# Two layers of a gated cross-attention block: Toeplitz rows of four heads read straight from kernel_rev, and two units with memory of their own

## The reference, cut to what matters

```python
def _L0_xattn_ref(k, v, q, ssm_kernel, D, head_dim):       # k = v = ctx, q = layernorm(x)
    kv = jnp.einsum('bhil,bhjl->bijhl', k_, v_)
    y = irfft(rfft(kv, n=fft_size) * rfft(ssm_kernel, n=fft_size))[..., :L]
    out = y + kv * D[None, None, None, :, None]
    out = jnp.einsum('bijhl,bhil->bjhl', out, q_)
...
x = x + jnp.tanh(g_xattn[0]) * _L0_xattn_ref(ctx_2048, ctx_2048, _layernorm(x), ssm_kernel, D, 8)
x = x + jnp.tanh(g_ffn[0]) * _L0_ffn_ref(_layernorm(x), ...)
x = x + jnp.tanh(g_xattn[1]) * _L1_xattn_ref(_layernorm(x), ctx_2048, mask)
x = x + jnp.tanh(g_ffn[1]) * _L1_ffn_ref(_layernorm(x), w_fc, w_proj)      # square(relu(x w_fc)) w_proj
```

## Time and profile before

| | |
|---|---|
| median of 3 runs | 231.15 us (230.76 to 231.24) |
| the profiled execution | 230.63 us, span of its instructions 228.9 us |
| TensorE busy | 217.5 us, 95% of the span, 1405 matmuls |
| VectorE busy | 177.5 us, 78% |
| ScalarE, GpSimd busy | 111.2 us, 49%; 77.7 us, 34% |
| granted TensorE clock, mean | 0.989 |
| DMA | 14068 packets, 11.46 MB |

### The profile page before, as it was taken

The page is one execution under the profiler, slowest core; times in us unless marked ns, Lnnn a source line. Parts: engine busy times, 40 slices in busy tenths (PEclk is TensorE's granted clock), DMA queues, the critical chain, the costliest instruction groups (busy, mean ns, idle before and its releaser), DMA issues.

```text
span 228.9 us, 4229 instructions
## 1 busy us (share of the span) xinstructions
PE 217.5 (95%) x1405; PEld 198.7 (87%) x1405; DVE 177.5 (78%) x507; ACT 111.2 (49%) x221; POOL 77.7 (34%) x113
## 2 busy tenths in 40 slices
PE   7679899999999999999999999999999999998994
PEld 7579899998889889889889898889989988998883
DVE  4289999988989978698986597873587638846874
ACT  2341367942355343746353573494932682435443
POOL 2279998376553321010130343200101211201530
PEclk9799999999999999999999999999999999999998
DMA  5699953000000007000000000000000100001011
GB/s 170 138 292 345 325 172 111 3 0 3 0 1 3 0 0 229 3 1 0 3 0 0 3 0 0 3 3 0 0 3 0 46 0 3 0 6 44 0 47 46
DMA packets 14068, 11.46 MB, mean 50 GB/s; under 512 B 2944, under 2 KB 13792, under 8 KB 14048
## 3 DMA queue, kind: packets, MB, share of 16 engines
q1 hardware_dynamic: 11792, 11.03, 15.7%
q10 hardware_dynamic: 2256, 0.18, 0.7%
HBM read 10.14 MB, written 1.07 MB: 49 GB/s over the span
## 4 chain that ended last, share of the span: by engine, by line
PE 76%; DMA 8%; DVE 8%; ACT 2%; POOL 2%; issue 2%; ACTq 0%; SPq 0%; DVEq 0%; POOLq 0%
PE bank L808 25%; PE bank L646 12%; PE bank L838 6%; PE bank L812 4%; PE bank L873 4%; PE bank L889 4%; PE bank L836 3%; PE bank L693 3%; DMA ctx<-in_ctx_rows 3%; PE bank L694 3%; PE bank L695 3%; DMA lag_rows<-lags 2%; PE bank L639 2%; DMA toe<-lag_rows 2%; PE bank L725 1%
## 5 line engine op out<-in xcount | busy, mean ns | idle before, releaser
L808 PE MATMUL bank<-w_split,xt 128*128 128x512 f32 (+1 forms) x288 | 66.3, 378 | 0.0
L808 PEld LDWEIGHTS bank<-w_split,xt 128*128 128x128 f32 x288 | 51.5, 188 | 7.0 <-issue 0.2
L1352 DVE SCALAR_TENSOR_TENSOR act<-silu,scal,bank 128x176 f32<-128x176 f32 (+2 forms) x80 | 23.7, 355 | 17.1 <-ACT silu L1044 17.1
L1044 ACT ACTIVATE silu<-bank 128x512 f32<-128x512 f32 (+1 forms) x24 | 13.5, 563 | 28.8 <-PE bank L812 28.7
L838 PE MATMUL bank<-d_split,a_t 128*128 128x512 f32 x70 | 24.9, 396 | 0.0
L1513 POOL TENSOR_TENSOR fold<-prod 128x512 f32<-128x512 f32 x16 | 20.7, 1296 | 11.6 <-DVE att L1211 7.6
L898 ACT ACTIVATE a_t<-bank 128x512 fp32r<-128x512 f32 (+1 forms) x24 | 13.4, 559 | 19.8 <-PE bank L646 16.4
L561 POOL TENSOR_TENSOR kv<-ctx_ext 128x640 f32<-128x640 f32 x15 | 19.5, 1306 | 9.7 <-ACT ctx_ext L898 4.0
L836 PE MATMUL bank<-d_split,a_t 128*128 128x256 f32 x77 | 20.5, 281 | 0.0
L1454 POOL TENSOR_SCALAR ve<-mv 128x2 f32<-128x2 f32 (+2 forms) x11 | 3.1, 280 | 49.6 <-DVE mv L1134 49.6
L1099 DVE TENSOR_TENSOR a_t<-bank,a_t 128x512 fp32r<-128x512 f32 (+1 forms) x24 | 15.3, 639 | 3.5 <-ACT a_t L898 3.5
(11 more groups left out here) (162 smaller groups left out, 466.3 us busy)
## 6 DMA issues: line engine op xcount, KB each, us to landing
toe<-lag_rows SPq DMA_DIRECT2D x3, 512.0 KB, 7.5
ring<-in_down_p SPq DMA_DIRECT2D x2, 704.0 KB, 5.0
ctx<-in_ctx_rows SPq DMA_DIRECT2D x2, 512.0 KB, 6.7
ring<-in_gate_p SPq DMA_DIRECT2D x2, 512.0 KB, 7.1
ring<-in_up_p SPq DMA_DIRECT2D x2, 512.0 KB, 5.9
out_x<-x_res SPq DMA_DIRECT2D x3, 256.0 KB, 2.1
tern_w<-in_w_fc SPq DMA_DIRECT2D x1, 640.0 KB, 4.4
tern_w<-in_w_proj SPq DMA_DIRECT2D x1, 640.0 KB, 5.6
```

What stands on the lines that cost most here:

```text
L808: pe.matmul(psum((name, b, c))[:, 0:w_cols], lhs, w_split[:, w, kt, part, cols], start=i == 0, stop=False)
L1044: drain(act_e.activation(silu[:, n % 2, 0:w_cols], psum(("gate", b, c))[:, 0:w_cols], ACT.Silu), ("gate", b, c))
L1352: drain(dve.scalar_tensor_tensor(out=act[:, whole], in0=silu[:, n % 2, here], scalar=scal[:, b, g:g + 1], in1=psum(("up", b, c))[:, here], ...
```

## The change

It does five things.

1. `toe` of heads 0 to 3 (`DIRECT = 2` groups of two heads) is read from `kernel_rev` itself and without waiting. DVE adds D to it afterwards: `add_skip(k)` takes the identity with its columns reversed, times D of the head (`skip_all`, a new load to all partitions), plus the half of `toe` that holds lag zero. `add_skip(0)` stands on DVE ahead of the first norm, `add_skip(1)` behind its kv 0 0. The twelve other heads go the old way.
2. Loads are moved: gate0 and gate1 of the ring stand behind heads 4 to 7 and 8 to 11; `mu` and the router's weights are issued by ScalarE after its part of turn_q 0 0. `lags` is loaded ahead of `skip_sb`.
3. GpSimd's kv 0 1 waits for DVE's kv 0 0, and its first fold for the store of `lag_rows`.
4. Units 3 and 4 get `hid_late` and `x1t_late` of their own, in the memory of `w_split`, and wait for the last chunk instead of for the unit before.
5. `TIMES` has new numbers. Up to the first products the list now has conv 0 0 to 0 5 ahead of the first `turn_w`, and then turn_w gate 0 to 3 in a row; mu_hi and mu_lo stand around conv 0 12; turn_ctx 1 0 stands after turn_w up 3; the third keep (4 matmuls) stands ahead of mask_up up 1 and no longer after conv 1 2. At the end hidden 2 1 stands ahead of down 7, turn_p 3 ahead of the statistics of unit 4, read 3 ahead of turn_0 4, turn_1 4 between hidden 3 1 and 3 2, all hidden pieces of unit 4 ahead of out 3, and the last keep behind out 4.

```diff
+DIRECT = 2
...
+LATE_UNIT = 3
...
-    "weights": [13, 20, 28, 30, 36, 37, 45, 55, 56, 57, 58, 61, 62, 67, 68, 69, 72, 75, 80, 87, 88, 101, 123, 125,
-        126, 127, 137],
...
-    "mu": [14, 15],
-    "mix1": [50, 53, 70, 83, 91, 93],
-    "kv0": [12, 19, 29, 32, 41],
-    "conv0": [16, 17, 21, 22, 24, 26, 33, 34, 38, 39, 47, 48, 51, 59, 63, 65],
-    "gather0": [25, 31, 44, 46, 54, 64, 76, 77],
...
-    "keeps": [74, 81, 106, 109, 110, 322],
...
-    "unit2": [262, 263, 266, 268, 273, 276, 277, 278, 280, 292, 299, 303, 309],
-    "unit3": [282, 285, 290, 295, 300, 304, 307, 308, 311, 315, 316, 319, 323],
-    "unit4": [297, 298, 302, 306, 310, 312, 313, 314, 321, 324, 326, 328, 330],
...
-    "low2": [294, 301, 305],
-    "low3": [317, 318, 320],
-    "low4": [325, 327, 329],
+    "weights": [26, 27, 28, 29, 33, 42, 44, 45, 51, 52, 63, 64, 65, 66, 67, 72, 73, 74, 82, 91, 92, 103, 122, 123,
+        127, 128, 138],
...
+    "mu": [48, 50],
+    "mix1": [56, 57, 75, 83, 94, 95],
+    "kv0": [19, 20, 23, 36, 40],
+    "conv0": [12, 13, 15, 16, 18, 21, 30, 31, 34, 37, 39, 46, 49, 60, 62, 68],
+    "gather0": [24, 25, 35, 41, 54, 55, 77, 78],
...
+    "keeps": [58, 76, 81, 109, 110, 330],
...
+    "unit2": [261, 262, 266, 269, 273, 279, 280, 281, 287, 292, 295, 301, 309],
+    "unit3": [284, 286, 289, 296, 298, 302, 305, 306, 311, 315, 317, 319, 328],
+    "unit4": [299, 300, 307, 308, 310, 312, 313, 314, 318, 322, 324, 325, 329],
...
+    "low2": [293, 303, 304],
+    "low3": [316, 320, 321],
+    "low4": [323, 326, 327],
...
-            assert at["out", u - 1] < at["hidden", u, 0]
+            if u < LATE_UNIT:
+                assert at["out", u - 1] < at["hidden", u, 0]
+            else:
+                assert at["hidden", u - 1, 2] < at["hidden", u, 0] and at["hid_lo", u - 1, 2] < at["hid_lo", u, 0]
+                assert at["chunk", B - 1, NPART - 1] < at["turn_1", u]
...
-    w_split = sb("w_split", [P, 2, 2, 2, GI], F32R)
+    split_at = region(4 * 8 * GI)
+    w_split = sb("w_split", [P, 2, 2, 2, GI], F32R, split_at)
...
+    hid_late = [sb(f"hid_late{k}", [P, JT, 2, P], F32R, split_at + 4 * JT * 2 * P * k) for k in range(2)]
+    x1t_late = [sb(f"x1t_late{k}", [P, 2, 2, P], F32R, split_at + 4 * JT * 4 * P + 4 * 4 * P * k) for k in range(2)]
+    hid_of = [hid_t, hid_t, hid_t] + hid_late
+    x1t_of = [x1t, x1t, x1t] + x1t_late
...
+    skip_all = sb("skip_all", [P, HEADS])
...
+    skip_spread, toe_skip = sem("skip_spread"), sem("toe_skip")
...
-            ring_load(0)
-            sp.wait_ge(lags_stored, 16)
             for k, hs in enumerate(TOE_LOADS):
...
-                src = bass.AP(lag_rows.tensor, hs.start * KPAD, [[1, P], [KPAD, len(hs)], [1, 256]])
+                if k == DIRECT:
+                    sp.wait_ge(lags_stored, 16)
+                rows = kernel_rev if k < DIRECT else lag_rows
+                src = bass.AP(rows.tensor, hs.start * KPAD, [[1, P], [KPAD, len(hs)], [1, 256]])
                 sp.dma_start(toe[:, hs.start:hs.stop, :], src).then_inc(toe_loaded[k], 16)
-                if k == 2:
-                    ring_load(1)
+                if k >= DIRECT and k < DIRECT + 2:
+                    ring_load(k - DIRECT)
             ring_load(2)
...
                     if half == 0:
-                        pe.wait_ge(toe_loaded[next(k for k, hs in enumerate(TOE_LOADS) if h in hs)], 16)
+                        k = next(k for k, hs in enumerate(TOE_LOADS) if h in hs)
+                        if k < DIRECT:
+                            pe.wait_ge(toe_skip, k + 1)
+                        else:
+                            pe.wait_ge(toe_loaded[k], 16)
...
-                                                 fc_t[:, kt, j * P:(j + 1) * P], x1t[:, part, kt, 0:n],
+                                                 fc_t[:, kt, j * P:(j + 1) * P], x1t_of[u][:, part, kt, 0:n],
...
-                                                 hid_t[:, j, part, k * P:(k + 1) * P],
+                                                 hid_of[u][:, j, part, k * P:(k + 1) * P],
...
+            act_e.dma_start(lags[:, :], kernel_rev).then_inc(lags_loaded, 16)
             act_e.dma_start(skip_sb[:, :], skip.unsqueeze(1)).then_inc(lags_loaded, 16)
-            act_e.dma_start(lags[:, :], kernel_rev).then_inc(lags_loaded, 16)
+            act_e.dma_start(skip_all[:, :], skip.partition_broadcast(P)).then_inc(skip_spread, 16)
...
             act_e.wait_ge(lags_made, 1)
             act_e.dma_start(lag_rows, lags[:, :]).then_inc(lags_stored, 16)
-            act_e.dma_start(router_w[:, :], gate_w).then_inc(small_loaded, 16)
-            for kt in range(2):
-                act_e.dma_start(mu[:, kt, :].rearrange("p (g s) -> p g s", g=NG),
-                                mask_up_w[:, kt * P:(kt + 1) * P, :].rearrange("g h s -> h g s")).then_inc(mu_loaded, 16)
...
+                    if step == ("turn_q", 0, 0):
+                        for kt in range(2):
+                            act_e.dma_start(mu[:, kt, :].rearrange("p (g s) -> p g s", g=NG), mask_up_w[:, kt * P:(kt + 1) * P, :]
+                                            .rearrange("g h s -> h g s")).then_inc(mu_loaded, 16)
+                        act_e.dma_start(router_w[:, :], gate_w).then_inc(small_loaded, 16)
...
-                        wait_filled(act_e, ("hidden", u - 1, 2))
+                        wait_filled(act_e, ("up", B - 1, NPART - 1) if u >= LATE_UNIT else ("hidden", u - 1, 2))
...
-                    drain(copy(x1t[:, 0, :, 0:n], psum(step)[:, 0:2 * n].rearrange("p (t n) -> p t n", t=2)), step)
+                    drain(copy(x1t_of[u][:, 0, :, 0:n], psum(step)[:, 0:2 * n].rearrange("p (t n) -> p t n", t=2)), step)
...
-                        wait_filled(act_e, ("out", u - 1) if u else ("turn_proj", 2))
-                    act_e.activation(hid_t[:, j0:j0 + nj, 0, 0:rows], relu[:, n % 2, 0:nj * rows].rearrange(
+                        wait_filled(act_e, ("up", B - 1, NPART - 1) if u >= LATE_UNIT else ("out", u - 1) if u else
+                                    ("turn_proj", 2))
+                    act_e.activation(hid_of[u][:, j0:j0 + nj, 0, 0:rows], relu[:, n % 2, 0:nj * rows].rearrange(
...
+
+            def add_skip(k):
+
+                dve.wait_ge(toe_loaded[k], 16)
+                for h in TOE_LOADS[k]:
+                    last = dve.scalar_tensor_tensor(out=toe[:, h, P:2 * P], in0=ident[:, ::-1], scalar=skip_all[:, h:h + 1],
+                                                    in1=toe[:, h, P:2 * P], op0=ALU.mult, op1=ALU.add)
+                last.then_inc(toe_skip, 1)
...
                 elif kind == "norm" and not by_scalar(*step[1:]):
...
+                    if n == 0:
+                        dve.wait_ge(skip_spread, 16)
+                        add_skip(0)
...
                     make_kv(dve, half, g).then_inc(kv_beside, 1)
+                    if half == 0 and g == 0:
+                        add_skip(1)
...
-                    residue(x1t[:, 1, :, 0:n], step, psum(step)[:, 0:2 * n].rearrange("p (t n) -> p t n", t=2),
-                            x1t[:, 0, :, 0:n])
+                    residue(x1t_of[step[1]][:, 1, :, 0:n], step, psum(step)[:, 0:2 * n].rearrange("p (t n) -> p t n", t=2),
+                            x1t_of[step[1]][:, 0, :, 0:n])
...
-                    dve.tensor_tensor(hid_t[:, j0:j0 + nj, 1, 0:rows],
+                    dve.tensor_tensor(hid_of[u][:, j0:j0 + nj, 1, 0:rows],
...
-                                      hid_t[:, j0:j0 + nj, 0, 0:rows].bitcast(F32), ALU.subtract).then_inc(hid_lo, 1)
+                                      hid_of[u][:, j0:j0 + nj, 0, 0:rows].bitcast(F32), ALU.subtract).then_inc(hid_lo, 1)
...
+                    if half == 0 and g == 1:
+                        pool.wait_ge(kv_beside, 1)
                     make_kv(pool, half, g).then_inc(kv_made, 1)
                 elif kind == "fold":
...
+                    if n == 0:
+                        pool.wait_ge(lags_stored, 16)
```

20 lines of the change are left out of this document (10 added, 10 removed), and 26 rows, old and new, of the table TIMES.

## The result

The changed kernel takes 231.62 us (median of 8 runs, 230.89 to 232.09), the kernel before 230.44 us beside it. The ratio is 1.0052, with a 95% interval of 1.0028 to 1.0076: slower by 1.2 us. The profiled execution took 231.89 us with a span of 230.1 us.

The account below looks back on a forecast made before the run. DVE, without slack from 20 to 28 us behind a hollow start, was taken as the bound up to the logits. Start +0.3 and end -0.35 gave -0.05 us: no change, median 231.1 us, range 229.6 to 232.7.

Parts of the forecast that it names:

- the 9.2 us transfer: First new transfer, Toeplitz rows of heads 0 and 1 (256 KB) behind ctx, forecast to land at 9.2 us.
- the start: Everything up to the logits: gains and new waits of DVE were summed to +0.3 us, bounds -0.5 and +1.3.
- The rest: Everything behind the first chunk; the only term forecast there was the one for the end, -0.35 us.
- the clock: Rival: a new PE hole from 10.3 to 11.3 us keeps TensorE at 1.2 GHz longer; 232.6 us, chance 0.04.
- owed mu_lo: DVE work done in the old start's hollow, still to be done later; about 0.43 us instead of 0.78.
- PE's wait ahead of gate tiles 2 and 3: Tiles need ring load 1, in near 19.5 us; PE idles 1 us or more there, DVE 0.4 us.
- Exclusion: Rival: DVE's adds and GpSimd's kv exclude each other, all DVE work 1.1 us late; 232.2 us, chance 0.2.
- DVE's adds need no semaphore by then: Reason for leaving the hold-up by GpSimd's kv (up to 1.25 us) out of the sum: GpSimd must still receive one.
- the moved small loads would cost: Rival: mu and router loads push the full DMA, ctx of half 1 or ring load 1 1.2 us later; 232.3, chance 0.13.
- DVE is not the limit: Rival: PE keeps its 0.9 us lead at the start and the tail gives 0.35; 229.9 us, chance 0.25.
- The term for the end: Units 3 and 4 and the work around the last down step: -0.35 us, bounds -1.1 and +0.3.
- The waits that I listed: New waits at the end: PE for the qt copy 0.5 us, hidden 4 0 for the copy of x1t 0.3 us.

Follow-up runs that it names:

- spread_pe: Changed kernel with D spread over the partitions on chip (identity scaled by D, matmul with ones) instead of by the skip_all load; ratio to the kernel before 0.9990.
- after_warm: Changed kernel with 13 more warm matmul steps ahead of the first turn of ctx and 4 ahead of turn_q; ratio to the kernel before 1.0038.
- adds_first: Changed kernel with the second pair of adds ahead of DVE's kv 0 0 instead of behind it; ratio to the kernel before 1.0050.
- loads_back: Changed kernel with the loads of mu and router weights back directly behind the taps' write on ScalarE's queue; ratio to the kernel before 1.0055.
- tail_only: Kernel before, with the changed order from down 3 (step 225) on and the own memory of units 3 and 4; ratio to the kernel before 0.9983.
- middle_only: Kernel before, with the changed order only between the first chunk (step 137) and down 3 (step 225); ratio to the kernel before 1.0006.
- mended_ring: spread_pe with both pairs of adds between norm mix 0 and kv 0 0, and ring load 0 ahead of the taps' write wait; ratio to the kernel before 0.9938.

## Why the prediction was wrong

**The step that failed** is the sentence that the new load of skip_all "is waited for by the same instruction as the 9.2 us transfer, which hides it". That is true of it as a wait and false of it as traffic. I priced its bytes at nothing, and let ctx land at 8.5 us and the new transfers behind it at 9.2 and 9.9. They landed at 9.34, 9.99 and 10.95 us, and the taps' write at 10.76 instead of 10.06. In the kernel before the load alone costs 1.5 us, which is more than the whole measured difference.

**The balance.** By the ratios the start costs 0.91%, 2.1 us; without the load (changed kernel to spread_pe, 0.62%) 1.4 us of that go, and 0.7 us stay, for +0.3 forecast. The rest gains 0.4 to 0.8%, 0.9 to 1.9 us, for -0.35 forecast. I put the cost of the start too low and the gain of the rest too low. The two errors partly cancel, and it is luck that 231.62 us lies inside my range of 229.6 to 232.7.

**The start, step by step.** A pair of adds takes 0.61 us (0.65 forecast), and the first pair starts when its rows land, as forecast, but at 10.09 and not at 9.2 us. Norm ends at 11.99 (11.25), turn_q starts at 12.05 (11.3), conv 0 0 at 13.81 (12.7): 0.75 us from the landing, the rest from the clock, since turn_q took 1.97 us and not 1.4. The second pair took 1.66 us. The copy of q_ext ended at 15.70 us (13.9). DVE's owed mu_lo was to cost 0.43 us; it took 1.21, beside GpSimd's fold, in the timeline of the changed kernel:

```profile
32.36 1.21 DVE L1147 TENSOR_TENSOR mu<-mu,mu 128x256 fp32r<-128x256 f32 x1
```

PE's wait ahead of gate tiles 2 and 3 did not appear; it did in after_warm, where PE came to them earlier.

**The rivals.** Exclusion and the clock, given 0.2 and 0.04, both happened, and neither decides: take away the first (adds_first) and the clock holds DVE up; take away both (after_warm, ratio 1.0038, interval down to 1.0005) and the ring loads do. I had argued against exclusion that DVE's adds need no semaphore by then. The first add of the second pair indeed went through; the second started within 0.01 us of GpSimd's kv and took 1.40 us. The Trainium skill (SBUF — State Buffer, section "SBUF: two separate sides") says that whichever of the two starts first keeps the ports for its whole instruction; the traces agree on the whole instruction: the add took 1.40 us beside a kv of 1.25, and in after_warm, where it was the add that went through, the kv took 1.46. Which of them was first they don't resolve. That the moved small loads would cost (0.13) is refuted by loads_back. That DVE is not the limit (0.25) is half right: in the changed kernel it is busy for all of 20 to 28 us, but in after_warm and the kernels behind it PE and DVE wait for ring loads, so DVE and the DMA bound the start together. And the early ring load, which gains 0.7 us, shows that the DMA's share of it counts.

**The end.** The term for the end was about right, and a gain in front of it was put at nothing. The last update of x_res starts 14.76 us after the last down step (15.2 forecast; 16.49 before, and 16.05 to 16.06 in four other profiles with the old tail). The waits that I listed are there, 0.5 us each for qt and x1t_late, and nothing is left of the wait for hid_t. But in tail_only the way from the first chunk to the end of down 7 grew by as much, to 151.01 us for 149.65 to 149.80, so the tail alone gives nothing in its trace. Behind the new order of the middle it gives 0.3 us (165.06 in middle_only, 164.7 to 164.9 with both), for -0.35 forecast. What I had missed is the middle: 165.77 to 165.06 us, -0.7. Its cause is open, since PE's visible gaps on this way sum to only 0.14 us in the kernel before and to nothing in middle_only. Forecast -0.35 for all, measured -1.37 us in the first pair of profiles and -1.0 us over all.

**What stays open.** Why the 16 engines are less busy beside 128 reads of 64 bytes. The runs show that they are, not which part of the way is clogged. Also, what else delays the last part of ctx, which lands anywhere between 6.1 and 8.9 us with the old start and no such load. Also, where the 0.7 us come from that the start costs without the load. The best version kept the old start and took only the rest (0.9919); whether a start with direct heads can beat it wasn't found, since mended_ring (0.9938) overlaps it.

## What to carry to other kernels

Price every new load twice: when it lands, and what it does to the loads around it. A small load that spreads one row over 128 partitions, issued into the first microseconds, can cost more than the work that it feeds (here 1.4 to 1.5 us); a matmul with ones does the same on chip. And before a start is made earlier, ask what else ends there: here three waits of nearly the same height (adds, clock, ring loads) stood one behind the other, and taking the first two away only uncovered the third. And know how typical the profiled execution is before two profiles are compared: two pairs of profiles hid a gain of 0.7 us that the times of all executions show.
